# A vision tower kernel: three groups of images in its triangular solves, their later columns on POOL, and the layer norms of one phase applied by ACT

## The chip, the cores and the metric

The kernel runs on one core of one Trainium2 chip. The metric is the device time of one execution in microseconds (us), as the median of several runs; less is better. The core has five engines that run side by side and meet only at semaphores: TensorE (PE; its weight loads are PEld), VectorE (DVE), ScalarE (ACT), GpSimd (POOL) and SyncE (SP, which here only issues DMAs). Each takes its own instructions strictly in order, so an instruction that waits holds up everything behind it on its engine.

## What is computed

64 images of 36 patches and a class token, so 37 tokens each, of width 256, go through an embedding, multi-query attention, an entmax-gated two-layer product network (`cp_mumoe`), a delta-rule attention and a mixture of 8 experts, each behind a layer norm:

```python
h = _L0_tok_ref(x, ...)
h = h + _L0_attn_ref(_layernorm(h), ...)
h = h + _L0_ffn_ref(_layernorm(h), ...)
h = h + _L1_attn_ref(_layernorm(h), ...)
h = h + _L1_ffn_ref(_layernorm(h), ...)
```

The part that the change touches is in `_L1_attn_ref`. For each image and each of two heads it needs the inverse of a unit lower triangular matrix of 37x37:

```python
A0 = jnp.tril(-(jnp.einsum('bhnid,bhnjd->bhnij', k_beta, k) * L[None, :, None]), -1)
M = eye - A0
A = solve_triangular(M, jnp.broadcast_to(eye, M.shape), lower=True, unit_diagonal=True)
v = A @ v
```

There are 128 such systems, one for an image and a head.

## The kernel before

Tokens are handled in tiles of three images (111 rows of SBUF), 22 tiles in 11 pairs. The phases run one after the other: embedding and first attention in turns over the pairs; the entmax gates; a **merged phase**; an **attended phase**, in the same block without a barrier; routing; and the experts.

A turn i of the merged phase runs, over a pair of tiles, the two-layer product network of pair i, its output and the statistics of the norm for pair i-1 (`add_outputs`), POOL's power for the norm (`power_rows`), the norm itself (`normalise`, on VectorE, L1319), the transposes, and for pair i-2 the products of the delta rule: `decay_products` on VectorE (L1328, L1333) writes the masked system of a tile, and `fold` on POOL (L1528, L1529) brings it to 111x74. VectorE begins a turn with `gate_second` and `gate_first` (L1291, L1283). SP stores every folded tile to DRAM (`n_rows`, L970).

The systems are solved by **groups** of images (`GROUPS`), since a solve wants one system to a partition and so needs a trip through DRAM: `load_systems` brings the folded systems of a group to `sys_n`, VectorE solves them into `sys_x` by forward substitution, `store_inverses` (L1000) writes the inverses to DRAM and `load_inverses` (L1008) brings them back in the layout of tiles. There are two groups, pairs 0 to 5 and 6 to 10, and one place for both. `sets` is the number of times that the systems of a group fit in 128 partitions: with two sets, each partition solves every second column of the inverse.

`substitution` (L1340) is a generator that emits one matrix row i of the solve at a time: a product of the finished part of each column with row i (L1383), then a reduce (L1390). Columns are cut in two parts, early and late, each with its own semaphore, and the products of both stand ahead of the reduces of both. `advance` puts rows between the other work of VectorE until an estimated cost, `SLOTS`, is used up. Group 0 is solved within merged turns 8 to 12, and is drained there before the last decay products. Group 1 is solved within the attended phase, and drained before tile 12.

In the attended phase, turn t runs on TensorE `solve_values(t)` (L1130, the inverse of tile t by its values), `read_out(t-1)`, `turn_outputs(t-3)`, `attend(t)` and `router_logits(t-3)`. `solve_values(t)` needs `spread_inverses(t)` of POOL (L1537), which needs the loaded inverses. VectorE adds the result to the tokens and takes the statistics (`add_read`, L1417 to L1425), POOL raises to the power -0.5 (`power_outputs`, L1547), and VectorE applies the norm (`normalise_outputs`, L1432) at the head of its turn. SP stores the finished tiles to `x_rows`. SP's queue also carries the expert weights: 8 MB to `arena_w1` behind the first `load_inverses`, and 4 MB to half of `arena_w2` behind the second.

The buffers of these phases are carved out of two arenas, `arena_w1` and `arena_w2`, and of `work`; the names in the rows are those of the arenas.

## Time and profile before

| what | value |
|---|---|
| median of 3 runs | 836.15 us (834.35 to 836.52) |
| the profiled execution | 836.92 us, its span 835.1 us |
| PE, PEld busy | 678.3 us (81%), 519.5 us (62%) |
| DVE, POOL, ACT busy | 448.1 us (54%), 260.3 us (31%), 229.1 us (27%) |
| mean granted clock of TensorE | 0.886 of full speed |

The page of the profile cuts the span in 40 slices of 20.9 us. Each digit is the busy share of an engine in tenths; PEclk is the granted clock of TensorE in tenths of full speed (2.4 GHz; 0.5 is 1.2 GHz):

```profile
PE   5899999999977149999983385196569999999994
DVE  1567777777765742444799199466613333333321
ACT  0223333333322043443431022032013232232321
POOL 2344444444441012455453122022012221222211
PEclk9899999999986558999997589578569999999998
```

The merged phase stands from slice 15 to slice 22, the attended phase in slices 23 to 28, and the experts behind slice 30. A time in a row of the trace is in us from the start of the span.

### The profile page before, as it was taken

How to read it: one execution, taken by the hardware profiler on the slowest of the kernel's cores; microseconds unless marked ns; L12 is line 12 of the kernel's file. 1: busy time of each engine (PE TensorE's matmuls, PEld its weight loads, DVE VectorE, ACT ScalarE, POOL GpSimd, SP SyncE). 2: the span in 40 equal slices, each digit the busy share in tenths (PEclk: the TensorE clock that was granted, in tenths of full speed). 3: DMA queues.
4: the chain of work that ended last, by engine and by line, in shares of the span. 5: the costliest groups of instructions: out<-in, count | busy, mean ns of one | idle time of the engine just before them, and what ended most of it. 6: DMA issues, size and time to landing. Idle time of an engine off the chain costs nothing. (4 is left out here: it accounts for less than half of the span.)

```text
span 835.1 us, 13690 instructions
## 1 busy us (share of the span) xinstructions
PE 678.3 (81%) x4562; PEld 519.5 (62%) x4562; DVE 448.1 (54%) x1266; ACT 229.1 (27%) x635; POOL 260.3 (31%) x418
## 2 busy tenths in 40 slices
PE   5899999999977149999983385196569999999994
PEld 4567677777755139999972364085436767667673
DVE  1567777777765742444799199466613333333321
ACT  0223333333322043443431022032013232232321
POOL 2344444444441012455453122022012221222211
PEclk9899999999986558999997589578569999999998
DMA  8211111111000000000100670193411111111110
GB/s 303 93 35 34 34 35 34 34 35 33 2 2 1 0 2 0 7 7 6 25 7 4 171 303 1 27 356 96 196 50 39 57 47 50 57 44 52 51 32 20
DMA packets 24643, 49.77 MB, mean 60 GB/s; under 512 B 15284, under 2 KB 15414, under 8 KB 23936
## 3 DMA queue, kind: packets, MB, share of 16 engines
q1 hardware_dynamic: 20960, 34.43, 12.7%
q0 software_dynamic: 3328, 10.23, 4.0%
q10 hardware_dynamic: 288, 4.25, 1.3%
q8 instruction: 39, 0.64, 0.3%
q14 instruction: 28, 0.23, 0.1%
HBM read 39.03 MB, written 9.86 MB: 59 GB/s over the span
## 5 line engine op out<-in xcount | busy, mean ns | idle before, releaser
L1762 PE MATMUL psum<-arena_w,work 128*128 x208 | 95.9, 605 | 1.0 <-DVE work L1814 1.0
L1860 ACT ACTIVATE work<-psum,cst 128x128 f32<-128x128 f32 x208 | 56.6, 383 | 144.1 <-PE psum L1775 144.1
L1786 PE MATMUL psum<-arena_w,work 128*128 x416 | 94.2, 379 | 0.4 <-ACT work L1860 0.4
L1786 PEld LDWEIGHTS psum<-arena_w,work 128*128 128x128 f32 x416 | 77.1, 190 | 10.5 <-issue 1.1
L1724 POOL DMA_INDIRECT out<-work,row_i x26 | 25.8, 990 | 160.2 <-DVE work L1836 160.2
L1823 DVE COPY work<-psum 128x512 f32<-128x512 f32 x52 | 36.0, 692 | 70.0 <-PE psum L1762 61.9
L346 PE MATMUL psum<-arena_w 128*111 128x256 f32 x264 | 64.1, 396 | 4.9 <-DMA arena_w<-in_pack 4.9
L1762 PEld LDWEIGHTS psum<-arena_w,work 128*128 128x128 f32 x208 | 38.3, 194 | 40.1 <-issue 40.1
L711 POOL TENSOR_TENSOR arena_w<-arena_w,work 101x592 f32<-101x592 f32 x33 | 39.6, 1200 | 72.2 <-DVE work L577 72.2
L346 PEld LDWEIGHTS psum<-arena_w 128*111 128x111 f32 x264 | 46.5, 183 | 19.7 <-issue 9.6
L1130 PE MATMUL psum<-tokens,work 111*111 111x128 f32 x88 | 18.2, 340 | 43.4 <-POOL work L1537 43.4
L1830 DVE TENSOR_TENSOR tokens<-psum,cst 128x256 f32<-128x256 f32 x26 | 11.0, 425 | 73.6 <-PE psum L1786 73.6
L702 POOL TENSOR_TENSOR arena_w<-arena_w 128x296 f32<-128x296 f32 x66 | 44.0, 689 | 20.7 <-DVE arena_w L545 20.7
L400 PE MATMUL psum<-arena_w 128*37 128x296 f32 x264 | 41.3, 434 | 3.3 <-ACT arena_w L665 3.3
L1130 PEld LDWEIGHTS psum<-tokens,work 111*111 111x111 f32 x88 | 13.7, 216 | 44.6 <-POOL work L1537 33.0
L1069 PE MATMUL psum<-arena_w 128*128 128x222 f32 x176 | 40.9, 379 | 0.5 <-DVE arena_w L1283 0.5
L634 ACT COPY arena_w<-psum 37x592 f32<-37x592 f32 x33 | 25.2, 765 | 58.1 <-PE psum L411 58.1
L557 DVE TENSOR_REDUCE work<-psum 101x16 f32<-101x592 f32 x33 | 25.4, 771 | 24.1 <-PE psum L400 24.1
L1069 PEld LDWEIGHTS psum<-arena_w 128*128 128x128 f32 x176 | 34.3, 202 | 5.3 <-issue 3.0
L1717 POOL DMA_INDIRECT tokens<-x_rows,row_i x26 | 25.5, 980 | 36.5 <-SPq L174 28.9
L411 PEld LDWEIGHTS psum<-cst,arena_w 101*128 101x128 f32 x264 | 26.4, 148 | 16.8 <-POOL arena_w L711 9.1
L432 PE MATMUL psum<-arena_w 37*32 37x74 f32 x1056 | 24.9, 231 | 13.5 <-DVE arena_w L568 12.2
(216 smaller groups left out, 1344.6 us busy)
## 6 DMA issues: line engine op xcount, KB each, us to landing
arena_w<-in_w SPq DMA_DIRECT2D x2, 4096.0 KB, 13.3
arena_w<-in_x SPq DMA_DIRECT2D x22, 333.0 KB, 2.9
x_rows<-tokens SPq DMA_DIRECT2D x22, 192.0 KB, 5.7
arena_w<-in_pack ACTq DMA_DIRECT2D x1, 2420.0 KB, 10.9
cst<-in_packc ACTq DMA_DIRECT2D x1, 1727.0 KB, 14.9
arena_w<-in_pack SPq DMA_DIRECT2D x1, 818.5 KB, 7.3
arena_w<-in_pack SPq DMA_DIRECT2D x2, 384.0 KB, 4.6
work<-a_rows SPq DMA_DIRECT2D x21, 32.4 KB, 2.0
```

Source lines behind the costliest of these rows:

```text
L346: mm = nc.tensor.matmul(bank[0][0:R, j * D:(j + 1) * D], xp[j][:, k * R:(k + 1) * R], w_lin[:, k, :], start=(k == 0), stop=(k == PC - 1))
L400: mm = nc.tensor.matmul(bank[4 + f][e * HP:e * HP + TOK, 0:HH * TOK], qt[:, a:a + TOK], kb[p % 2 * 2 + e], start=True, stop=True)
L411: mm = nc.tensor.transpose(turns_bank[:, c * 128:c * 128 + PR], prob[p % 2][:, c * 128:(c + 1) * 128], ident[0:PR, 0:PR])
L702: nc.gpsimd.tensor_tensor(kb[p % 2 * 2 + e].rearrange("p (h s) -> p h s", h=HH), kt[:, a:a + TOK].unsqueeze(1).broadcast_to([128, HH, TOK] ...
L711: nc.gpsimd.tensor_tensor(by_head(prob[p % 2], HP), by_head(prob[p % 2], HP), small[p % 2][:, 2 * NH:3 * NH].unsqueeze(2).broadcast_to([PR ...
L1069: mm = nc.tensor.matmul(bank[2 + f // 2 % 2][:, (f % 2) * W:(f % 2 + 1) * W], w_out1[:, f, :], z1, start=True, stop=True)
L1130: mm = nc.tensor.matmul(bank[t % 2][0:R, h * 128:(h + 1) * 128], ab[t % 2][:, h * R:(h + 1) * R], x_half(t)[:, h * 128:(h + 1) * 128], sta ...
L1724: pool.indirect_dma_start(out_h, bass.IndirectOffsetOnAxis(ap=row_i[:, 2 * i + j:2 * i + j + 1], axis=0), yo[j], None).then_inc(y_stored[j ...
L1762: mm = nc.tensor.matmul(bank[2 * j + f][:, :], xgt[j][:, k * 128:(k + 1) * 128], arena_w1[:, bass.ds(expert * (2 * FF) + (k * FF + f * 512 ...
L1786: mm = nc.tensor.matmul(bank[7][:, 0:D], ht[j][:, g * 128:(g + 1) * 128], arena_w2[:, bass.ds(expert * (FC * D) + g * D, D)], start=(g == ...
L1823: nc.vector.tensor_copy(hp[j][:, f * 512:(f + 1) * 512], bank[2 * j + f][:, :]).then_inc(h_out[j], 1)
L1860: nc.scalar.activation(ht[j][:, g * 128:(g + 1) * 128], bank[4 + f][:, k * 128:(k + 1) * 128], ACT.Gelu, bias=cst[:, bass.ds(expert * FC + ...
```

## The change

- `GROUPS` has three groups: pairs 0 to 4, 5 to 7 and 8 to 10 (30, 18 and 16 images; 2, 2 and 4 sets). Each has a place of its own (`place_of`), so a solve need not wait until the group before it has been stored.
- The columns of a solve are cut at column 16. The earlier ones stay on VectorE, as products and reduces of one part only. The later ones are solved on POOL by columns: for each i from 16 on, a product of the solved x[i] with column i of the system and an addition to all the later rows. Both engines call the same `substitution`, each with its own semaphore; `solved` of a group is complete when both have reported.
- `SLOTS` has new budgets, three for VectorE and two for POOL, with a new estimate of a row's cost. POOL must empty its queue before it spreads the first tile of a group.
- Both norms are applied by ACT, as x times a scale plus a bias; POOL makes the bias (minus mean times scale) behind its power. VectorE keeps the statistics.
- SP stores and reloads group 0 ahead of the stores of tiles 19 to 21, and group 1 ahead of the 8 MB of weights. The loaded inverses lie in `arena_w2`.

```diff
-GROUPS = ((0, 6), (6, PAIRS))
-SLOTS = (1.0, 1.0, 5.0, 1.7)
+GROUPS = ((0, 5), (5, 8), (8, PAIRS))
+SLOTS = (1.0, 5.5, 1.0, 4.0, 1.2)
...
+            def substitution(eng, ops, g, which):
...
+                for i in range(which * split * sets, TOK - which):
+                    most = min(cols, i // sets + 1)
+                    c0, c1 = (split, most) if which else (0, min(split, most))
+                    if c0 >= c1 or i == which == 0:
+                        continue
+                    j0, j1 = (i + 1, TOK) if which else (0, i + 1)
...
+                    free(eng, chain[which], steps[which])
+                    if which:
+                        ops.tensor_tensor(w, x[:, c0:c1, i:i + 1].broadcast_to(shape),
+                                          n[:, j0:j1, i].unsqueeze(1).broadcast_to(shape), ALU.mult).then_inc(chain[which], 1)
+                        eng.wait_ge(chain[which], steps[which] + 1)
+                        ops.tensor_tensor(x[:, c0:c1, j0:j1], x[:, c0:c1, j0:j1], w, ALU.add).then_inc(chain[which], 1)
+                    else:
+                        ops.tensor_tensor(w, x[:, c0:c1, j0:j1], n[:, i, j0:j1].unsqueeze(1).broadcast_to(shape),
+                                          ALU.mult).then_inc(chain[which], 1)
+                        eng.wait_ge(chain[which], steps[which] + 1)
+                        ops.tensor_reduce(x[:, c0:c1, i], w, AX_X, ALU.add).then_inc(chain[which], 1)
...
-                    if g:
-                        store_inverses(g - 1)
+                        if t == NT - NB and g == LAST > 0:
+                            store_inverses(0)
+                            load_inverses(0)
                     load_systems(g)
-                for g in range(LAST):
+                for g in range(1, LAST):
+                    store_inverses(g)
                     load_inverses(g)
...
+                        last = nc.scalar.activation(xn[i % 2][:, j * D:(j + 1) * D], h_pair(i)[:, j, :], ACT.Identity,
+                                                    bias=st1[:, 16 + j:17 + j], scale=st1[:, 14 + j:15 + j])
...
                 for t in range(NT + 3):
                     copy_solved(t)
+                    normalise_outputs(t - 2)
                     copy_turned(t - 3)
                     copy_attended(t)
...
                 for t in range(NT + 3):
-                    if t == firsts[LAST]:
-                        advance(math.inf)
-                    normalise_outputs(t - 2)
+                    turn_no[0] = PAIRS + 2 + t
+                    while t in firsts and len(queue) > LAST - firsts[t]:
+                        solve_some(0.1)
                     add_read(t - 1)
                     keep_logits(t - 3)
                     if t > 0:
-                        advance(SLOTS[3])
+                        solve_some(SLOTS[2])
...
                 for t in range(-2, NT + 1):
                     power_outputs(t - 1)
+                    if t + 2 in firsts:
+                        take_up(math.inf, firsts[t + 2])
+                        while queue:
+                            solve_some(0.1)
                     spread_inverses(t + 2)
+                    take_up(PAIRS + 2 + t)
+                    solve_some(SLOTS[4])
```

How the rows of the solve now stand on VectorE, at the end of group 0 in merged turn 10. Before, two rows of the solve (each two products, then two reduces; 72 partitions):

```order
L1383 TENSOR_TENSOR work<-arena_w 72x560
L1383 TENSOR_TENSOR work<-arena_w 72x361
L1390 TENSOR_REDUCE arena_w<-work 72x16
L1390 TENSOR_REDUCE arena_w<-work 72x19
L1383 TENSOR_TENSOR work<-arena_w 72x576
L1383 TENSOR_TENSOR work<-arena_w 72x400
L1390 TENSOR_REDUCE arena_w<-work 72x16
L1390 TENSOR_REDUCE arena_w<-work 72x20
```

Now (124 partitions, two sets), followed by the decay products:

```order
L998 TENSOR_TENSOR work<-arena_w 124x288
L1001 TENSOR_REDUCE arena_w<-work 124x8
L998 TENSOR_TENSOR work<-arena_w 124x296
L1001 TENSOR_REDUCE arena_w<-work 124x8
L1401 TENSOR_TENSOR arena_w<-psum,arena_w 111x222
```

The late part has left VectorE, so each product is followed at once by the reduce that needs it.

POOL between the last fold of the merged phase and the first spread of an inverse (`spread_inverses`, 111x222). Before:

```order
L1528 TENSOR_TENSOR arena_w<-arena_w 111x74
L1529 TENSOR_TENSOR arena_w<-arena_w 111x74
L1537 TENSOR_TENSOR work<-work,arena_w 111x222 x3
```

Now, where "..." leaves out eleven pairs of the same kind:

```order
L1553 TENSOR_TENSOR arena_w<-arena_w 111x74
L993 TENSOR_TENSOR work<-arena_w 100x52
L996 TENSOR_TENSOR arena_w<-arena_w,work 100x4x13
...
L993 TENSOR_TENSOR work<-arena_w 100x10
L996 TENSOR_TENSOR arena_w<-arena_w,work 100x10
L1005 ISA
L1561 TENSOR_TENSOR work<-arena_w 111x222 x3
```

Thirteen rows of group 1 and the mark that it is solved (L1005) have moved between the two.

POOL in attended turn 8, between the power of tile 7 (L1572) and the spread of tile 10. Before, the power and the spread stood next to each other, as in every turn:

```order
L1547 TENSOR_TENSOR work<-work 111x1
L1537 TENSOR_TENSOR work<-work,arena_w 111x222
```

Now, where "..." leaves out nine pairs:

```order
L1572 TENSOR_TENSOR work<-work 111x1
L1573 TENSOR_SCALAR work<-work 111x1
L993 TENSOR_TENSOR arena_w<-arena_w 128x33
L996 TENSOR_TENSOR arena_w<-arena_w 128x3x11
...
L993 TENSOR_TENSOR arena_w<-arena_w 128x5
L996 TENSOR_TENSOR arena_w<-arena_w 128x5
L1005 ISA
L1561 TENSOR_TENSOR work<-arena_w 111x222
```

Eleven rows of group 2 stand ahead of the spread of the first tile of group 1.

## Rows read from the trace of the kernel before

**Rows 1.** Busy by stretch: PE, PEld, DVE, ACT, POOL, PEclk, DMA share, GB/s.
```profile
440.00:474.00 34.00, 8.48 (x30) 5.92 (x30) 21.84 (x54) 3.00 (x15) 10.55 (x26) 0.61 0.22 42
```

**Rows 2.** Timeline (start, us, engine, line, [idle <-releaser]): attended phase begins.
```profile
473.54 1.16 PE L1130 MATMUL psum<-tokens,work 111*111 111x128 f32 x4 [11.28 <-POOL work L1537]
...
478.96 1.00 DVE L1417 SCALAR_TENSOR_TENSOR tokens<-psum,arena_w,tokens 111x256 f32<-111x256 f32 x2 [15.73 <-PE psum L1151]
```

**Rows 3.** Timeline: the trip of the second group's inverses, SP and TensorE.
```profile
531.18 2.01 SPq L1000 DMA_DIRECT2D a_rows<-arena_w  x4
538.20 3.31 SPq L1008 DMA_DIRECT2D work<-a_rows  x7
...
540.63 0.88 PEld L1130 LDWEIGHTS psum<-tokens,work 111*111 111x111 f32 x4 [25.19 <-POOL work L1537]
```

**Rows 4.** Timeline: VectorE, starts of merged turns and fixed work in one.
```profile
388.43 0.45 DVE L1291 SCALAR_TENSOR_TENSOR arena_w<-psum,arena_w 128x222 f32<-128x222 f32 x1 [4.25 <-PE psum L1081]
...
400.13 0.45 DVE L1291 SCALAR_TENSOR_TENSOR arena_w<-psum,arena_w 128x222 f32<-128x222 f32 x1 [4.24 <-PE psum L1081]
...
415.00 0.37 DVE L1328 TENSOR_TENSOR arena_w<-psum,arena_w 111x222 f32<-111x222 f32 x1
...
417.57 0.40 DVE L1383 TENSOR_TENSOR work<-arena_w 72x90 f32<-72x90 f32 x2
...
438.38 0.43 DVE L1291 SCALAR_TENSOR_TENSOR arena_w<-psum,arena_w 128x222 f32<-128x222 f32 x1
```

**Rows 5.** Timeline: VectorE, solve rows with one part and with two (x2).
```profile
409.63 0.19 DVE L1383 TENSOR_TENSOR work<-arena_w 72x36 f32<-72x36 f32 x1
...
410.15 0.21 DVE L1383 TENSOR_TENSOR work<-arena_w 72x49 f32<-72x49 f32 x1
...
528.36 0.73 DVE L1383 TENSOR_TENSOR arena_w<-arena_w 120x288 f32<-120x288 f32 x2
...
529.63 0.74 DVE L1383 TENSOR_TENSOR arena_w<-arena_w 120x296 f32<-120x296 f32 x2
```

**Rows 6.** Groups: line, engine, op, shapes, count | busy us, mean ns | idle.
```profile
L1383 DVE TENSOR_TENSOR arena_w<-arena_w 120x296 f32<-120x296 f32 x1 | 0.5, 457 | 0.0
...
L1432 DVE TENSOR_SCALAR tokens<-tokens,work 111x256 f32<-111x256 f32 x22 | 11.0, 502 | 16.6 <-POOL work L1547 16.6
...
L1319 DVE TENSOR_SCALAR arena_w<-tokens,arena_w 111x256 f32<-111x256 f32 x22 | 8.1, 411 | 5.9 <-POOL arena_w L1489 5.9
...
L1237 ACT COPY tokens<-psum 111x256 f32<-111x256 f32 x22 | 8.1, 366 | 0.0
```

**Rows 7.** Timeline: POOL, short operations of one merged turn.
```profile
332.14 0.20 POOL L1514 TENSOR_TENSOR arena_w<-arena_w 111x2 f32<-111x2 f32 x1
...
333.30 0.31 POOL L1528 TENSOR_TENSOR arena_w<-arena_w 111x74 f32<-111x74 f32 x1 [0.53 <-DVE arena_w L1333]
333.69 0.33 POOL L1529 TENSOR_TENSOR arena_w<-arena_w 111x74 f32<-111x74 f32 x1
```

**Rows 8.** Timeline: a VectorE product of the solve, and POOL beside it.
```profile
449.69 1.01 DVE L1383 TENSOR_TENSOR work<-arena_w 72x512 f32<-72x512 f32 x2
449.86 0.90 POOL L1515 TENSOR_TENSOR arena_w<-arena_w 111x2 f32<-111x2 f32 x1
```

**Rows 9.** Timeline: VectorE, one turn of the attended phase up to its solve.
```profile
498.51 1.00 DVE L1417 SCALAR_TENSOR_TENSOR tokens<-psum,arena_w,tokens 111x256 f32<-111x256 f32 x2
...
500.37 0.33 DVE L1383 TENSOR_TENSOR arena_w<-arena_w 120x51 f32<-120x51 f32 x2
```

**Rows 10.** Timeline: VectorE, add_read behind the restart, and the last two.
```profile
548.11 1.00 DVE L1417 SCALAR_TENSOR_TENSOR tokens<-psum,arena_w,tokens 111x256 f32<-111x256 f32 x2 [1.36 <-PE psum L1151]
...
552.64 1.00 DVE L1417 SCALAR_TENSOR_TENSOR tokens<-psum,arena_w,tokens 111x256 f32<-111x256 f32 x2 [1.36 <-PE psum L1151]
...
574.02 0.99 DVE L1417 SCALAR_TENSOR_TENSOR tokens<-psum,arena_w,tokens 111x256 f32<-111x256 f32 x2
...
576.88 1.00 DVE L1417 SCALAR_TENSOR_TENSOR tokens<-psum,arena_w,tokens 111x256 f32<-111x256 f32 x2
```

More of the change, by code:

```diff
@@ L952, in group_of, with place_of, products_of @@
                 return im0, im1, nb, stride, 128 // stride
+            def place_of(g):
+                if g == LAST:
+                    return (arena_w2[:, k * TOK * TOK:(k + 1) * TOK * TOK] for k in range(2))
+                if g == 0:
+                    return sys_n, sys_x
+                return (arena_w1[:, k * TOK * TOK:(k + 1) * TOK * TOK] for k in range(2))
+            def products_of(g):
+                space = arena_w2[:, 2 * TOK * TOK:] if g == LAST else work
+                return space[:, 0:16 * TOK], space[:, 16 * TOK:16 * TOK + 21 * 21]
             def systems_of(rows, g, h):
@@ new lines, in advance @@
+            def advance(queue, budget, fixed, each):
+                while queue and budget > 0:
+                    size = next(queue[0], None)
+                    if size is None:
+                        queue.pop(0)
+                    else:
+                        budget -= fixed + each * size
+            steps = [0, 0]
+            begun = {}
+            ends = {GROUPS[g][1] - 1: g for g in range(len(GROUPS))}
+            firsts = {2 * GROUPS[g][0]: g for g in range(len(GROUPS))}
@@ L1393, in substitution @@
-                    for which in range(2):
-                        dve.wait_ge(chain[which], steps[which])
-                    nc.vector.engine_nop().then_inc(solved[g], 1)
-                pending = [None]
-                def advance(budget):
-                    while pending[0] is not None and budget > 0:
-                        cost = next(pending[0], None)
-                        if cost is None:
-                            pending[0] = None
-                        else:
-                            budget -= cost
+                    nc.vector.memset(rows_n[:, 0:TOK * TOK:TOK + 1], 1.0).then_inc(diagonal[g], 1)
@@ L1408, in add_read, with solve_some, all_steps @@
+                    dve.wait_ge(diagonal[g], 1)
+                queue = []
+                turn_no = [0]
+                def solve_some(budget):
+                    advance(queue, budget, 0.3, 0.0021)
+                def all_steps(g):
+                    begun[g] = turn_no[0]
+                    prepare(g)
+                    yield 700
+                    yield from substitution(dve, nc.vector, g, 0)
                 def add_read(t):
@@ L1546, in power_outputs, with solve_some, take_up, all_steps @@
                     pool.wait_ge(vare2, t + 1)
-                    tt(ve2[t % 2][:, 1:2], ve2[t % 2][:, 0:1], halves[:, 0:1], ALU.pow).then_inc(powered2, 1)
+                    free(pool, normed2, t - 1)
+                    link(tt(ve2[t % 2][:, 1:2], ve2[t % 2][:, 0:1], halves[:, 0:1], ALU.pow))
+                    ts(ve2[t % 2][:, 2:3], st2[t % 2][:, 6:7], ve2[t % 2][:, 1:2], -1.0, ALU.mult, ALU.mult).then_inc(powered2, 1)
+                queue = []
+                def solve_some(budget):
+                    advance(queue, budget, 0.5, 0.0042)
+                taken = []
+                def take_up(turn, most=LAST):
+                    for g in range(most + 1):
+                        if g not in taken and begun[g] < turn:
+                            taken.append(g)
+                            queue.append(all_steps(g))
+                def all_steps(g):
+                    pool.wait_ge(diagonal[g], 1)
+                    yield from substitution(pool, nc.gpsimd, g, 1)
                 ends_of_groups = [2 * p1_ - 1 for _, p1_ in GROUPS[:LAST]]
```

145 lines of the change are left out of this document (59 added, 86 removed).

## The prediction, before the changed kernel was run

> **What bounds the kernel now.** I read the busy table by stretches first, then the engines in order of time with what ended their idle time. TensorE fills most of the span, but two holes stand in it. From 440 to 474 us it works 8.48 of 34 us at a granted clock of 0.61 [rows 1]; the last part of that hole ends with the first multiplication of the attended phase at 473.54, after 11.28 us of waiting for POOL [rows 2]. The second hole is the longer: 25.19 us, again ended by POOL's spread inverses [rows 3]. In both, POOL itself waits: for VectorE to finish a triangular solve and for its result to go to DRAM and back. That trip is in [rows 3]: stores issued at 531.18, loads at 538.20, TensorE going again at 540.63, so 9.4 us from solved to working. In between, VectorE sets the pace. A merged turn takes 11.70 us where TensorE bounds it (388.43 to 400.13); the next three, with a solve in them, take 38.25 us together, 3.15 more than three such turns [rows 4].
>
> **What the solve costs on VectorE.** Before, a row of the solve has two independent parts (early and late columns), so each covers the other's latency. A row with one part runs product, reduce, next product strictly in turn: 0.52 us for 36 elements (409.63 to 410.15) [rows 5]. The product alone grows from 0.19 us at 36 elements [rows 5] to 0.457 at 296 [rows 6], 0.00103 us an element. A row with one part of n elements is then 0.45 + 0.00206 n us. A row with both parts, 288 and 200 elements, took 1.27 us [rows 5]; the same row with its first part alone comes to 0.45 + 0.59 = 1.04. The change takes 41% of that row's elements away from VectorE and, by this, 18% of its time. On short rows it saves nothing.
> Two groups before: 12472 and 6653 elements, both parts counted, come with 0.25 us a row (what is left of 1.27 after 488 x 0.0021) to about 36 and 24 us. After: 36 rows in each of three groups with 5315, 5315 and 2687 elements in the first part, so 27.1, 27.1 and 21.7 us, 76 against 60. The norms give back 8.1 + 11.0 = 19.1 us [rows 6]. VectorE's total load stays nearly level; what can be won is only the place of the work and the two trips to DRAM.
>
> **The norms on ACT.** Nearest row: an ACT copy of 111x256 at 0.366 us [rows 6]; 44 of them are 16 us on an engine that worked 3.00 of 34 us [rows 1]. They stand behind a wait for POOL's power in ACT's order, with the GELUs of the turn's second half queued behind. The two new POOL scalings cost about 0.3 us each with their gap [rows 7]. I count this at nothing: between 0 (VectorE's slack covers it) and 0.5 us for each of 11 turns.
>
> **The merged phase after.** POOL's part of a solve is 20 rows of two operations. Start to start POOL needs 0.39 us for 74 elements and about 0.28 for 2 (0.20 and the 0.08 gap seen behind the larger) [rows 7]: 0.275 + 0.0016 n, so 0.68 us a row at 43 elements, 13.6 us for a group of 30 or 18 images, 12.5 for the last. The Trainium skill (Perfetto Trace Analysis, GPSIMD Engine Instruction) says to time POOL by such spacing and not by reported durations; by the durations alone the row would be 0.5 us and the drains below a quarter shorter.
> VectorE's fixed work in a turn: gates 0.7, first decay products and outputs with their statistics 2.57 (415.00 to 417.57) [rows 4], second decay products 0.8 (estimate from the 0.37 of one and two smaller), 4.1 in all. The order puts 14, 11, 9 and 13 rows of the solve into turns 7 to 10, and two preparations of 1.3 us. That is 13.0, 12.8, 12.7 and 13.1 us, all above 11.7. To turns 9, 10 and 11 I add 0.7 each for the shared port: [rows 8] show POOL's 2-element product, 0.20 us elsewhere, taking 0.90 while a VectorE product of 512 elements ran. From 388.4 this leads to 441 for turn 11 (before 438.4), and with its 12 rows to 455. The last decay products then wait for POOL's strengths, which stand behind seven of POOL's solve rows; I put their end at 462, before 463.2. Almost no gain here.
> The trip of group 0 leaves early: POOL marks it solved behind its inverses of turn 11, at about 453.5, so its inverses are back at 463. But POOL does not spread them: its order empties the queue first, 13 rows of group 1 behind the last fold. 462 + 0.8 + 13 x 0.68 + 1.4 of port waits + 0.6 for the spread is 465 + 9: TensorE starts at **474**, against 473.54 [rows 2]. One wait takes the other's place.
>
> **The attended phase after.** The first add_read came 5.4 us after the start (478.96 after 473.54) [rows 2], so now at 479.4. A turn of VectorE is 1.86 us of add_read and logits [rows 9] plus its solve rows; the order gives 2, 2, preparation, 4, 4, 3, 3, 3 in turns 1 to 8: 28.7 us. In POOL's turn 8 stands the second drain: 11 rows of group 2, 7.3 us, ahead of the spread of tile 10. Tile 9's add_read comes 12.4 us behind tile 7's, not 7.2: 5.2 us lost. Then 16.4 us to tile 14 and 5.6 for the last rows; with 1 us for a lowered clock the last group is solved at 479.4 + 25.1 + 12.4 + 16.4 + 5.6 + 1 = 540. Eight smaller stores instead of four: I keep the 9.4 us of [rows 3], so TensorE restarts at **549**, 8.7 us later than before (540.63), with six tiles left and not ten.
> From a restart at the low clock turns take 4.53 us (548.11 to 552.64), later 2.86 (574.02 to 576.88) [rows 10], of which 0.3 was the norm in VectorE's chain: 2.7 now. Last add_read before: 36.25 us behind the restart. After: 3 + 2 x 4.53 + 4 x 2.7 = 22.9, so 571.9 against 576.88. The remaining path is unchanged. **Gain 5 us.** The profiled execution took 836.92 us (span 835.1), 0.8 above the median of 836.15; 831.9 for it, **831** for the median.
>
> **Bounds of what no row shows.** POOL's rows with broadcast, strided operands: from 0.5 us (durations) to 0.9 (each product behind half a VectorE product) instead of 0.68; 24 of them lie on the path, -4 to +5 us. The trip with eight stores: 7 to 12 us, -2 to +3. ACT's norms: 0 to +4.
>
> **Rivals.**
> The drains are hidden. If POOL runs well ahead in the merged phase, TensorE starts when group 0's inverses are back, 465, and the stall before tile 10 shrinks to 2 us: another 12 us, 819. For it: POOL works only 10.55 of 34 us in [rows 1]. Against: in the order both drains stand squarely ahead of the spreads, and the last fold cannot come before VectorE's decay products.
> The port decides. In [rows 8] we see a short POOL operation held for nearly all of a VectorE product. If each meeting is paid in full, VectorE loses a POOL operation, 0.28 us, for each of 27 rows in the merged turns (7.6, of which 2.1 are counted), and the 24 drained rows 0.2 to 0.3 more each: 5.5 + 6 us, and the result is 842, slower. It turns from gain to loss at 5 us of such waits. For it: now both engines run two-input products at once for some 40 us. Against: reduces, half of VectorE's rows, held nothing in these rows. The Trainium skill (SBUF — State Buffer, Who interferes with whom) has this as an exclusive lock: two-input VectorE operations and POOL's reads block each other for the whole instruction, reduces never do. The held operation agrees.
> Nothing comes of it. The last group's turns run 0.3 us slower each than I sum, and the restart is at 553: 835 to 838. A lowered clock through the attended phase does this too; [rows 1] show 0.61 behind a hole.
>
> **How the numbers follow.** Forecast 831 (825 to 834), 0.52; hidden drains 0.15; nothing 0.17; the port 0.16. About 0.3%, 2.5 us, can be told from no change: faster below 833.6, slower above 838.7. Some of the forecast's upper end belongs to no change: faster 0.66, same 0.17, slower 0.17. Range 821 to 840.
>
> **What would show it.** Right: merged turns of 13 us from turn 7; a POOL stretch of product and sum rows of 9 to 11 us just before its first spread, TensorE's first attended work at 474 +/- 3; a hole of 4 to 6 us before tile 10; a hole of about 14 us before tile 16 that ends near 549; single-part solve rows of 0.45 us plus size. Wrong: TensorE starting at 465 (drains cheap), VectorE products well above 0.46 us beside POOL (the port), or GELUs of the second half waiting for ACT's norm by more than 0.5 us a turn.

## The result, and the profile of the changed kernel

| | before | changed |
|---|---|---|
| median of 20 runs, us | 835.06 (830.57 to 836.71) | 839.56 (834.80 to 840.88) |
| ratio | | 1.0046, 95% interval 1.0031 to 1.0061 |
| profiled execution (span), us | 836.92 (835.1) | 839.81 (837.9) |
| busy VectorE, POOL, ACT, us | 448.1, 260.3, 229.1 | 431.4, 302.5, 246.7 |

The change makes the kernel 0.46% slower, where the forecast said 0.6% faster. Of its 20 executions 4 took 834.8 to 835.8 us and 16 took 838.0 to 840.9; the profiled one is of the second kind. Three moments of the trace carry what follows: TensorE's first attended work, the last add_read, and the issue of the next phase's weights, which marks the end of the attended phase.

VectorE's gate_second starts the merged turns, as in [rows 4]. Timeline of the changed kernel, VectorE (start, us, engine, line, operands, what ended its idle time):
```profile
389.43 0.45 DVE L1377 SCALAR_TENSOR_TENSOR arena_w<-psum,arena_w 128x222 f32<-128x222 f32 x1 [4.02 <-PE psum L1147]
...
394.05 0.09 DVE L1427 MEMSET arena_w<- 128x37 f32 x1 [2.38 <-DMA arena_w<-n_rows]
...
398.99 0.57 DVE L1406 SCALAR_TENSOR_TENSOR arena_w<-psum,arena_w 111x111 f32<-111x111 f32 x2 [1.86 <-POOL arena_w L1539]
...
406.68 0.44 DVE L1377 SCALAR_TENSOR_TENSOR arena_w<-psum,arena_w 128x222 f32<-128x222 f32 x1
...
413.38 0.57 DVE L1406 SCALAR_TENSOR_TENSOR arena_w<-psum,arena_w 111x111 f32<-111x111 f32 x2 [1.85 <-POOL arena_w L1539]
...
420.98 0.44 DVE L1377 SCALAR_TENSOR_TENSOR arena_w<-psum,arena_w 128x222 f32<-128x222 f32 x1
```
The first turn with a solve takes 17.25 us and not 13.0. Two waits stand in it: 2.38 us in the preparation, for the loads of group 0's systems, and 1.86 us before the second decay products, for POOL's strengths. The next turn takes 14.30, with the second wait again.

The preparation stood at the head of a turn in the kernel before too, and did not wait. VectorE before, and SyncE's loads of group 0's systems after:
```profile
401.56 1.20 DVE L1351 MEMSET arena_w<- 128x1369 f32 x1 [0.23 <-issue]
402.86 0.09 DVE L1356 MEMSET arena_w<- 128x37 f32 x1
```
```profile
388.92 1.67 SPq L1046 DMA_DIRECT2D arena_w<-n_rows  x4
```
Before, two loads were issued from 399.02, 1.1 us ahead of the turn that begins at 400.13, and VectorE went on with the decay products at 403.02. Now there are four, from 388.92, 0.5 us ahead of the turn at 389.43, and VectorE goes on at 394.05, 5.1 us behind the first issue.

POOL ahead of the first spread, and TensorE behind it, the counterpart of [rows 2]; timelines of POOL, TensorE and VectorE:
```profile
470.79 0.47 POOL L993 TENSOR_TENSOR work<-arena_w 100x52 f32<-100x52 f32 x1
471.35 0.29 POOL L996 TENSOR_TENSOR arena_w<-arena_w,work 100x52 f32<-100x52 f32 x1
471.71 0.43 POOL L993 TENSOR_TENSOR work<-arena_w 100x60 f32<-100x60 f32 x1
...
481.01 1.08 POOL L1561 TENSOR_TENSOR work<-arena_w 111x222 f32<-111x222 f32 x2 [0.15 <-POOL arena_w L996]
...
481.72 1.16 PE L1196 MATMUL psum<-tokens,work 111*111 111x128 f32 x4 [12.71 <-POOL work L1561]
...
487.14 1.00 DVE L1452 SCALAR_TENSOR_TENSOR tokens<-psum,arena_w,tokens 111x256 f32<-111x256 f32 x2 [11.12 <-PE psum L1217]
```
From 470.79 to 481.01 POOL does nothing but group 1's rows, 13 of them; the loads of group 0's inverses had been issued from 468.12 on, as the next lines show. TensorE starts 8.2 us later than before (473.54).

SyncE's queue through the attended phase, the counterpart of [rows 3], with TensorE's restart and VectorE's last work of the phase:
```profile
461.22 2.06 SPq L1064 DMA_DIRECT2D a_rows<-arena_w  x4
468.12 5.48 SPq L1072 DMA_DIRECT2D arena_w<-a_rows  x11
...
548.52 3.67 SPq L1064 DMA_DIRECT2D a_rows<-arena_w  x8
553.54 2.81 SPq L1072 DMA_DIRECT2D arena_w<-a_rows  x6
...
555.92 1.19 PE L1196 MATMUL psum<-tokens,work 111*111 111x128 f32 x4 [11.29 <-POOL work L1561]
...
556.39 0.46 SPq L1093 DMA_DIRECT2D arena_w<-in_w  x1
556.89 26.76 SPq L1097 DMA_DIRECT2D x_rows<-tokens  x44
...
582.22 0.17 DVE L1467 TENSOR_TENSOR work<-psum,cst 111x8 f32<-111x8 f32 x1 [1.65 <-PE psum L1236]
...
586.97 0.35 SPq L1643 DMA_DIRECT2D arena_w<-in_w  x1
```
All 44 stores of x_rows stand in SyncE's order behind the last group's inverses and 4 MB of weights. They are issued until 583.65, so VectorE's last work of the phase (582.22) is not its end: the next phase begins at 586.97. The last add_read was at 575.71 (before 576.88, [rows 10]), so 1.2 us were won up to there, and 4.6 lost behind it.

The attended phase holds one thing more, the turns behind the hole before tile 10; VectorE's add_reads:
```profile
525.24 1.00 DVE L1452 SCALAR_TENSOR_TENSOR tokens<-psum,arena_w,tokens 111x256 f32<-111x256 f32 x2 [6.62 <-PE psum L1217]
...
529.77 1.00 DVE L1452 SCALAR_TENSOR_TENSOR tokens<-psum,arena_w,tokens 111x256 f32<-111x256 f32 x2 [0.72 <-PE psum L1217]
...
534.30 1.00 DVE L1452 SCALAR_TENSOR_TENSOR tokens<-psum,arena_w,tokens 111x256 f32<-111x256 f32 x2 [1.50 <-PE psum L1217]
...
537.26 0.99 DVE L1452 SCALAR_TENSOR_TENSOR tokens<-psum,arena_w,tokens 111x256 f32<-111x256 f32 x2
```
Two turns take 4.53 us each, and the granted clock of TensorE is 0.50 from 525.2 to 534.3; then 2.96. In the traces of e2 and e7 below, which have the same hole of 10.1 us, the same two turns take 3.71 and 2.9 us at a granted clock of 0.97 and 0.96. So behind the same hole the clock differs from trace to trace, and 2.4 us between two of these traces can be the clock alone.

### The profile page after: what moved, and what is told of

Read it like the earlier page. It is cut to its first block and busy times, and to the rows that moved or that the text cites. A ratio compares the mean times of both kernels' runs of the same rounds, so it can differ in the third digit from the quotient of the medians.

```text
span 837.9 us, 13862 instructions
## 1 busy us (share of the span) xinstructions
PE 675.0 (81%) x4562; PEld 515.0 (61%) x4562; DVE 431.4 (51%) x1186; ACT 246.7 (29%) x679; POOL 302.5 (36%) x582
## 5 line engine op out<-in xcount | busy, mean ns | idle before, releaser
L1196 PE MATMUL psum<-tokens,work 111*111 111x128 f32 x88 | 17.6, 332 | 31.5 <-POOL work L1561 31.5
L634 ACT COPY arena_w<-psum 37x592 f32<-37x592 f32 x33 | 25.2, 763 | 57.9 <-PE psum L411 57.9
L1452 DVE SCALAR_TENSOR_TENSOR tokens<-psum,arena_w,tokens 111x256 f32<-111x256 f32 x44 | 21.2, 483 | 36.4 <-PE psum L1217 35.6
L411 PEld LDWEIGHTS psum<-cst,arena_w 101*128 101x128 f32 x264 | 26.2, 148 | 16.7 <-POOL arena_w L711 9.5
```

The costliest lines, as they stand in the source:

```text
L411: mm = nc.tensor.transpose(turns_bank[:, c * 128:c * 128 + PR], prob[p % 2][:, c * 128:(c + 1) * 128], ident[0:PR, 0:PR])
```

## The experiments

The ratio is that of each kernel to the kernel before, run beside it, with its 95% interval. The three last columns are from the profiled execution of each, counted from its first gate_second of the merged phase (before 320.69, changed 319.83), so that what happened earlier does not enter: TensorE's first attended work, the last add_read, the end of the phase. "Less" and "more" below are differences of medians, against the 839.56 of the changed kernel where nothing else is named. The kernels were run at different times, so where such a difference is small the two ratios and their intervals decide. The profiled execution of e1 is its fastest, 823.78, 4.5 us below its median.

| run | median us | ratio | attended start | last add_read | end |
|---|---|---|---|---|---|
| before | 835.06 | 1 | 152.9 | 256.2 | 262.9 |
| changed | 839.56 | 1.0046 (1.0031 to 1.0061) | 161.9 | 255.9 | 267.1 |
| e1 | 828.24 | 0.9909 (0.9888 to 0.9930) | 156.8 | 242.5 | 253.8 |
| e2 | 835.69 | 0.9996 (0.9976 to 1.0015) | 161.7 | 252.8 | 260.8 |
| e3 | 837.19 | 1.0021 (1.0002 to 1.0039) | 158.2 | 257.3 | 264.1 |
| e4 | 817.21 | 0.9784 (0.9761 to 0.9808) | 150.0 | 235.2 | 246.5 |
| e5 | 827.32 | 0.9915 (0.9892 to 0.9938) | 157.3 | 245.1 | 254.4 |
| e6 | 833.23 | 0.9982 (0.9965 to 0.9999) | 161.4 | 248.7 | 257.3 |
| e7 | 836.94 | 1.0040 (1.0023 to 1.0057) | 161.0 | 252.6 | 264.1 |
| e8 | 820.45 | 0.9834 (0.9813 to 0.9855) | 157.9 | 239.1 | 247.1 |
| e9 | 818.79 | 0.9801 (0.9787 to 0.9814) | 157.8 | 237.0 | 246.0 |
| e10 | 818.85 | 0.9801 (0.9786 to 0.9815) | 150.5 | 238.5 | 246.2 |
| e11 | 817.26 | 0.9775 (0.9750 to 0.9800) | 150.4 | 235.1 | 243.1 |
| e12 | 821.27 | 0.9839 (0.9824 to 0.9854) | 149.9 | 240.1 | 246.8 |
| e13 | 831.61 | 0.9960 (0.9941 to 0.9979) | 162.4 | 249.3 | 257.3 |
| e14 | 821.75 | 0.9840 (0.9826 to 0.9853) | 151.6 | 238.8 | 248.4 |
| e15 | 835.44 | 0.9999 (0.9989 to 1.0009) | 157.5 | 253.7 | 261.6 |

**e1, POOL's drains.** POOL empties its queue only up to the group that is about to be spread.
```diff
-                        while queue:
+                        while len(queue) > len(taken) - 1 - firsts[t + 2]:
                             solve_some(0.1)
```


> The changed kernel, but POOL empties its queue of solve rows ahead of a spread only as far as the group that is spread: group 1's rows no longer stand before the first spread (10.1 us from 470.79 to 480.9), group 2's no longer before tile 10 (6.9 us from 514.6). Theory A, the place of these rows in POOL's order is what costs: TensorE starts its attended work when group 0's inverses are back, 472 instead of 481.7, the hole before tile 10 falls to about 2 us, the last group is solved some 8 us earlier, and the time falls from 839.6 to about 831. Rival B, the rows cost as much wherever they stand (shared port, blocked products): the attended turns grow by what the drains gave, and the time stays within 2 us of 839.6.

Measured 828.24, 11.3 us less. The hole before tile 10 (10.10 us between two add_reads) is gone. The attended start moves by 5.1 us only, not 9.7: in POOL's order six rows of group 1 remain ahead of the first spread, those of its last merged turn. This is A, and 3 us more than it said: the two turns of 4.53 us are also absent from this trace. Without the drains the change is a gain of 0.9%, with them a loss of 0.5%.

**e2, stores earlier.** SyncE stores 12 tiles before it waits for the last group.
```diff
+                store_rows(range(12))
                 store_inverses(LAST)
                 load_inverses(LAST)
...
-                for t in range(NT):
+                store_rows(range(12, NT))
```


> The changed kernel, but SyncE stores the first 12 tiles of x_rows before it waits for the last group's solve, not after it and after the 4 MB of weights. Theory A, the last 4 us of the attended phase (last VectorE work 582.4, next phase 587.0) belong to this backlog of 44 stores: the phase ends at about 583 and the time falls by 4 us to 835.5. Rival B, the weights' own 4 MB or the last stores end it anyway: less than 1 us.

Measured 835.69, 3.9 us less, as A said; from the last add_read to the end it is 8.0 us, not 11.3. The last add_read is earlier too in this trace, by 3.1 us, and 2.4 of that is the clock (see above).

**e3, norms back on VectorE.** Both norms as in the kernel before.
```diff
+                    normalise(i - 1)
                     decay_products(i - 2, 1)
...
+                    normalise_outputs(t - 2)
                     add_read(t - 1)
```


> The changed kernel with both norms back on VectorE (0.50 us x 2 a merged turn, 0.41 us an attended turn), all else kept, three groups and POOL's columns too. Theory A, the norms on ACT are a gain where VectorE is late: four solving turns of the merged phase grow by 1 us each, 22 attended turns by 0.2 to 0.4, and the time rises by 4 to 8 us to 844 to 848. Rival B, ACT's norm costs more than it gives (11.85 us a turn instead of 11.70 where no solve runs, and a longer chain power, scaling, norm in each attended turn): the time falls by 1 to 4 us.

Measured 837.19, 2.4 us less: B, though only just, since the two ratios' intervals touch (1.0002 to 1.0039 and 1.0031 to 1.0061). The turns without a solve are 11.70 and not 11.85 us, and the first two gate_seconds stand 9.23 apart, not 10.35: 2 us before any solve. But the norm here also stands between the two decay products, where the changed kernel waits for POOL; e6, e12 and e15 tell this apart.

**e4, POOL's rows left out.** The later columns are not computed; POOL only marks them as solved.
```diff
-                for i in range(which * split * sets, TOK - which):
+                for i in range(which * split * sets, 0 if which else TOK):
```


> The changed kernel without POOL's share of the solve: the later columns are not computed, POOL only marks them done; VectorE's rows are all there. It gives the whole price of POOL's rows, their place in the order and their use of the shared port together. Theory A (place in the order): the time is at most 3 us below that of the kernel in which only the drains are put right, near 829. Theory B (the port): it is 8 us or more below it, and VectorE's solving turns of the merged phase fall from 14.3 and 14.6 us to 13 or less.

Measured 817.21, 11 us below e1, which A did not allow. But B's sign is missing: the merged turns take 17.41, 14.30, 14.19 and 14.06 us, against 17.25, 14.30, 14.63 and 14.66. POOL's rows lengthen a merged turn by 0.6 us at most, and VectorE's wait before the second decay products is 1.86 us without them too. What else made the 11 us was open; the waits in both traces pointed to the mark. SyncE's queue, the store of group 0's inverses, in e1 and then in e4:
```profile
458.32 2.06 SPq L1064 DMA_DIRECT2D a_rows<-arena_w  x4
```
```profile
453.59 2.16 SPq L1064 DMA_DIRECT2D a_rows<-arena_w  x4
```
Counted from the first gate_second (317.12 and 319.48) these are 141.2 and 134.1.

**e5, marked at once.** On top of e1, the mark stands behind the last row, not at the queue's next advance.
```diff
+                    if i == TOK - 1 - which:
+                        eng.wait_ge(chain[which], steps[which])
+                        ops.engine_nop().then_inc(solved[g], 1)
                     yield (c1 - c0) * (j1 - j0)
-                eng.wait_ge(chain[which], steps[which])
-                ops.engine_nop().then_inc(solved[g], 1)
```


> The kernel with the drains put right (828.2 us) and one thing more: each engine marks its share of a group as solved right behind its last row. Before, the mark came only when the queue was next advanced, on POOL a whole turn behind the last row (last row of group 0 ended at 449.0 in that trace, SyncE's stores followed at 458.3). Theory A, this late mark makes most of the 11 us between that kernel and the one without POOL's rows (817.2): stores of group 0 at about 451, TensorE's attended start 7 us earlier, time 820 to 822. Rival B, the difference is POOL's rows themselves (the port, and rows drained later beside VectorE): time within 2 us of 828.

Measured 827.32, B's time: theory A falls. The store now leaves at 454.27 (135.5 from the first gate_second, 5.7 earlier), and TensorE starts no earlier. POOL's timeline shows why:
```profile
469.81 0.33 POOL L1554 TENSOR_TENSOR arena_w<-arena_w 111x74 f32<-111x74 f32 x1
470.10 0.46 POOL L993 TENSOR_TENSOR work<-arena_w 100x52 f32<-100x52 f32 x1
...
475.11 0.30 POOL L996 TENSOR_TENSOR arena_w<-arena_w,work 100x56 f32<-100x56 f32 x1
475.37 0.56 POOL L1562 TENSOR_TENSOR work<-arena_w 111x222 f32<-111x222 f32 x1
```
The last fold is at 469.81, and six rows of group 1 (5.3 us) still stand between it and the spread. The trip through DRAM had not been what POOL waited for.

**e14, the last slot too.** As e5, and POOL takes no rows in its last merged turn.
```diff
-                    solve_some(SLOTS[3])
+                    if i <= PAIRS:
+                        solve_some(SLOTS[3])
```


> The kernel that marks at once (827.3 us) without POOL's own six rows at the end of its last merged turn (5.3 us of POOL just ahead of the first spread, 470.1 to 475.4 in that trace). Theory A, these rows took the place of the late mark: TensorE's attended work starts at 470.5 to 471 instead of 476.1, and the time falls by 4 to 6 us to about 822, near the 817.2 of the kernel without POOL's rows. Rival B, the shared port is the rest: less than 2 us gained.

Measured 821.75, 5.6 us less than e5: A. The attended start is at 151.6, against 150.0 without POOL's rows. So of the 11 us between e1 and e4, 6.5 are the place of POOL's marks and rows, and some 4.5 are left for the rows themselves, the port among them. That last figure is loose: by the ratios it is 4.7 us with about 2 either way, and in the two traces the phase ends only 1.9 us apart.

**e6, solve rows between.** VectorE's rows of a merged turn are split about the second decay products.
```diff
-SLOTS = (1.0, 5.5, 1.0, 4.0, 1.2)
+SLOTS = (1.0, 3.6, 1.0, 4.0, 1.2)
...
                     add_outputs(i - 1)
+                    solve_some(1.9)
                     decay_products(i - 2, 1)
```


> The changed kernel (839.6 us) with about four solve rows of each merged turn moved on VectorE to stand between the outputs and the second decay products, as such rows and the norm did in the kernel before; the rest of the rows follow as now. Theory A, the merged turns with a solve are long (14.3, 14.6 us against the 12.8 I summed) because VectorE idles 1.9 us there for POOL's strengths: those turns take 12.5 to 13 us and the time falls by 4 to 6 us to about 834.5. Rival B, POOL only reaches its strengths later because VectorE's rows stand ahead of its norm inputs or hold the port: turns stay at 14 us or more, time within 1.5 us of 839.6.

Measured 833.23, 6.3 us less: the size is A's, the path only half. The first two turns with a solve fall to 15.21 and 12.79 us and the fourth to 13.99, but the third grows to 15.37, since the first decay products now come before POOL's strengths. Timeline of VectorE in e6:
```profile
420.83 0.38 DVE L1401 TENSOR_TENSOR arena_w<-psum,arena_w 111x222 f32<-111x222 f32 x1
422.95 0.57 DVE L1406 SCALAR_TENSOR_TENSOR arena_w<-psum,arena_w 111x111 f32<-111x111 f32 x2 [1.74 <-POOL arena_w L1540]
```
POOL's seven solve rows of the turn before stand ahead of those strengths. The four turns together are 3.5 us shorter, yet the attended start is unchanged (161.4). Each of the two slots rounds up to a whole row, so VectorE does six rows more of group 1 ahead of its last decay products (up to the product of 256 elements, in the changed kernel up to 208), and POOL's last fold comes where it was: 150.1 from the first gate_second, in the changed kernel 150.7. The gain comes behind the start: the rows of groups 0 and 1 are done before the first add_read, the last group is begun earlier and solved 9.2 us earlier (540.44, counted from the first gate_second 219.5 against 228.7), and both holes shrink, from 10.10 to 7.36 and from 15.60 to 12.92 us.

**e7, preparation later.** Group 0 is prepared behind the second decay products of its turn.
```diff
-                    solve_some(SLOTS[0])
+                    if i - 3 != GROUPS[0][1] - 1:
+                        solve_some(SLOTS[0])
...
-                    solve_some(SLOTS[1])
+                    solve_some(SLOTS[1] + (1.8 if i - 3 == GROUPS[0][1] - 1 else 0))
```


> The changed kernel with the preparation of group 0 moved on VectorE from the head of turn 7 to behind that turn's second decay products, with the same number of rows behind it. In the changed kernel VectorE stands 2.4 us there for the loads of the systems while TensorE waits for its decay products (the turn takes 16.9 us). Theory A: the turn takes 14.5 us and the time falls by 2.4 us to 837.2. Rival B: the wait was covered, the turn keeps 16 us or more, time within 1 us of 839.6.

Measured 836.94, 2.6 us less in the medians, but the ratios, 1.0040 and 1.0046, have intervals that almost coincide: no gain is shown. The turn falls by 1.55 us to 15.70, between what A and B said, and turn 9 grows from 14.63 to 15.32, so the four turns are 0.8 us shorter together. Of the 3.0 us between the two traces at the phase's end, 2.4 is the clock.

**e13, the last three together.** e2, e6 and e7 in one, the drains kept.

> The changed kernel with the three things that the forecast had not priced taken away together (rows between outputs and second decay products, group 0 prepared late, 12 tiles stored early), POOL's drains kept. Theory A, they lie one behind the other on the path: 839.6 - 6.3 - 2.6 - 3.9 = 826.8. Rival B, the waits overlap (the earlier merged turns only lengthen POOL's drain, whose rows are then all still ahead of it): 831 or more.

Measured 831.61, 8.0 us less: B. The gains overlap. The attended start is at 162.4, where it was. The four merged turns are 2.5 us shorter, but the last fold is no earlier (151.0 from the first gate_second, 150.7 in the changed kernel): as in e6 VectorE has done more rows ahead of its last decay products. POOL's 13 rows follow the fold as before:
```profile
469.96 0.33 POOL L1561 TENSOR_TENSOR arena_w<-arena_w 111x74 f32<-111x74 f32 x1
470.24 0.57 POOL L993 TENSOR_TENSOR work<-arena_w 100x52 f32<-100x52 f32 x1
470.89 0.29 POOL L996 TENSOR_TENSOR arena_w<-arena_w,work 100x52 f32<-100x52 f32 x1
...
480.59 1.08 POOL L1569 TENSOR_TENSOR work<-arena_w 111x222 f32<-111x222 f32 x2 [0.15 <-POOL arena_w L996]
...
481.30 1.16 PE L1201 MATMUL psum<-tokens,work 111*111 111x128 f32 x4 [14.13 <-POOL work L1569]
```

**e8, all five together.** e5, e2, e6 and e7 in one kernel (e5 holds e1).

> The changed kernel with all of it: POOL empties its queue only as far as needed, marks at once, rows between outputs and second decay products, group 0 prepared late, x_rows of 12 tiles stored before SyncE waits for the last group. If the parts are independent and lie on one path: 839.6 - 11.3 (drains) - 7 (marks) - 5 (rows between) - 2.4 (preparation) - 3.9 (stores) = 810. If they overlap, since VectorE's load of 76 us of solve stays: 815 to 818.

Measured 820.45, 1.7% faster than before, but short of the sum by 10 us and of the cautious range by 2: the parts overlap more than either said.

**e9 to e11, where the rows go.** e9 is e8 with more rows in each attended turn; e10 is e9 with the rows ahead of the last decay products and of the first spread taken out; e11 is e10 with more rows still.
```diff
-SLOTS = (1.0, 3.6, 1.0, 4.0, 1.2)
+SLOTS = (1.0, 3.6, 1.6, 4.0, 2.0)
```


> The kernel with all five corrections (820.5 us) and one size changed: VectorE takes 1.6 instead of 1.0 of solve budget in an attended turn (3 rows instead of 2), POOL 2.0 instead of 1.2. In the trace of that kernel the last group is solved at 532.5, TensorE then stands 10 us for the trip through DRAM (add_reads 529.96 and 542.95). Theory A, the last hole costs its whole trip because the rows end only when the tiles before it are used up; rows taken two or three tiles earlier let tiles 13 to 15 cover the trip: hole 3 us or less, time 812 to 815. Rival B, VectorE's attended turns grow by just what is saved and the hole stays: within 2 us of 820.5.

Measured 818.79, within B's 2 us, though the hole is gone, as A said. Before tile 16 the largest gap is 4.53 us instead of 12.99, yet the last add_read comes only 2.1 us earlier: the attended turns have grown.

> As the kernel with 1.6 and 2.0 of budget, and besides no solve rows ahead of the last two decay products on VectorE (turn 12), half as many at the end of turn 11, and none of POOL's in its turn 12, ahead of the first spread (5.3 us, six rows, in the trace of the kernel that marks at once); the products get a place beside the router's logits, so that rows may run later. Theory A, after the drains were put right the attended start hangs on these rows: it moves from 17 us behind the inverses' store to 10, 5 to 7 us earlier, and since the rows left over run beside attended tiles the time falls by 3 to 6 us against the kernel without this. Rival B, VectorE's rows are only moved and the last group is solved later by as much: within 1.5 us.

Measured 818.85: B, though the attended start moves by 7.3 us, to 150.5. Rows not done by then are done later, a hole before tile 16 is back (8.39 us), and the last group is solved 0.5 us sooner at most.

> As the last, with 2.2 of budget for VectorE in an attended turn. Theory A: the hole before tile 16 is gone at 1.6 already and longer turns only delay the tiles before: 0 to 2 us slower. Rival B: the trip still shows at 1.6, and 2.2 gains 2 to 4 us more.

Measured 817.26, 1.6 us less than e10, where A had 0 to 2 more and B 2 to 4 less; the intervals of e10 and e11 overlap, so neither is shown. It is the fastest kernel of the study that computes everything: 0.9775 (0.9750 to 0.9800) of the kernel before, 2.2% faster.

**e12 and e15, the norms by themselves.** e12 is e10 with both norms back on VectorE, as in e3. e15 is the kernel before with both norms on ACT and nothing else changed.

> The kernel with corrections, 1.6 and 2.0 of budget and the free tail, with both norms back on VectorE. In the changed kernel this edit gave 2.4 us, but there the norm also covered the wait for POOL's strengths. Theory A, with that wait covered by solve rows the norms are worth having on ACT: the merged turns with a solve grow by 1 us each and the time rises by 3 to 6 us. Rival B, ACT's norm costs by itself (0.15 us in each merged turn without a solve, a longer chain in each attended turn): the time falls by 1 to 3 us.

> The kernel before with one part of the change alone: both norms applied by ACT, with POOL's scalings; two groups, all columns on VectorE, solve rows still standing between outputs and second decay products. Theory A, ACT's chain costs 0.15 us in each of 7 merged turns without a solve, and gives VectorE back 0.73 us in each turn with one and 0.4 in each attended turn with solve rows (44 norms, 19.1 us, of which VectorE's late turns are some 14): 3 to 6 us faster than before, 830 to 832. Rival B, what VectorE wins it waits for elsewhere: within 1.5 us of 835.5. Rival C, the longer chain power, scaling, norm costs in the last six attended turns: slower, 837 or more.

e12 measured 821.27, 2.4 us more than e10, in A's direction and short of its range. e15 measured 835.44, no change: B. In e15 the merged phase loses: 10.34 for 9.22 between the first two gate_seconds, 11.85 for 11.70 in each turn without a solve, and the turns with one 13.62, 13.11 and 13.39 for 13.05, 12.53 and 12.67. The attended phase wins 7.2 us (from start to last add_read 96.1 for 103.3), of which 1.8 is one turn of 4.53 us behind the restart where the kernel before has two; its end hands back 1.3: 8.0 us from last add_read to end, before 6.7. So the norm on ACT is a loss in the merged phase and a gain in the attended one; a kernel with the one and not the other was not run.

## Why the prediction was wrong

Its own sum for the profiled execution was 831.9; it took 839.81. Of these 7.9 us, 7.7 were lost up to the attended start, 3.9 won back up to the last add_read, and 4.6 lost behind it; the rest of the program was some 0.5 shorter.

- **Merged turns 7 to 10: 61 us, not 53 (turn 11 starts at 450.3 and not at 441; 1.0 of this was there at turn 7).** The step that failed is the count of VectorE's fixed work, 4.1 us a turn, and of its preparations, 1.3 us each, with no waits in them. The old order had solve rows and the norm between the first and second decay products [rows 4], and these covered POOL's power and strengths; the change takes both away. The price is 1.85 to 1.86 us in each of the four turns, 0.2 to 0.3 more before the first decay products of turns 9 and 10, and 2.38 once for loads that are now four and issued later against the turn: 10.3 us in all, while the rest of the four turns was 2.5 us shorter than I summed. 13.0 + 2.38 + 1.86 is the 17.25 measured. The diff showed that rows and norm were gone from between; I priced the instructions and not the waits they had covered. POOL's share by the port, 0.7 a turn in my sum, was 0.4 to 0.6 (e4).
- **From turn 11 to the attended start: 31.5 us, not 33.** The mechanism was right: POOL's 13 rows stood ahead of the spread, and took 10.2 us from 470.79 to 481.01, the 8.8 + 1.4 of the sum. That makes the attended start 481.7 for 474. I had called it "one wait takes the other's place"; e1, e5 and e14 show how deep this goes: drain, mark and last slot each have to go before the next one shows. The second drain took 6.9 us from 514.6 on, 7.3 forecast.
- **Attended start to last add_read: 94.0 us, not 97.9.** The drain before tile 10 is there (13.4 us between add_reads of tiles 7 and 9, 12.4 forecast). The trip with eight small stores took 7.4 us from first store to TensorE, not 9.4. The two turns of 4.53 us stood behind the hole before tile 10, where I had 1 us for the clock, and not behind the restart, where I had two of them: the first there took 2.76 (558.85 to 561.61). That the clock fell there and not here I can't explain, and e2 and e7 have it at neither place; this part of the sum came out near by luck.
- **Last add_read to the end: 11.3 us, not 6.7.** "The remaining path is unchanged" failed. With six tiles left at the restart and not ten, SyncE has less time for 44 stores and 4 MB behind the same wait. e2 gives the size: 3.9 us by the medians, 3.3 in the tail of its trace.

The waits are read from the trace, on the engine that sets the pace there; the runs show them less directly. e13 puts rows into them, prepares late and stores early, the drains kept, and takes 831.6 us, where the forecast was 831. But it does not get there by the forecast's path: its four merged turns are only 2.5 us shorter, its attended start is at 162.4 from the first gate_second, where the forecast had some 154, and it makes up for that behind the start. That the two times agree is in part luck. No run shows an attended start as early as 154 with the drains kept.

The **norms on ACT** were counted at nothing, with the bound of 0 to 4 us. The traces show 2 us lost in the merged phase before a solve begins. The sign that I had named, GELUs of the second half later by more than 0.5 us, is there in turn 7: the norm waits 3.17 us for POOL on ACT, and these GELUs begin 10.3 us into the turn, for 7.6 before; in a turn without a solve it is 0.4 us. The sizing row was wrong too: an ACT norm, whose scale and bias each come from a column of memory, takes 0.60 us, not the 0.37 of a copy. Groups of the changed kernel:
```profile
L1300 ACT ACTIVATE tokens<-tokens,work 111x256 f32<-111x256 f32 x22 | 13.2, 600 | 18.1 <-POOL work L1573 18.1
...
L1292 ACT ACTIVATE arena_w<-tokens,arena_w 111x256 f32<-111x256 f32 x22 | 12.0, 595 | 18.7 <-POOL arena_w L1511 18.7
```
The Trainium skill (ScalarE: Activation LUTs, What ACT_TABLE_LOAD costs) had this price: 186 ns and 0.833 ns an element, and some 93 ns for each such operand, which for 256 elements and two operands makes 585 ns, an estimate; the rows agree at 595 and 600. By that estimate the 44 norms are 26 us on ACT; the rows above have 25.2 busy, and my sum had 16.

Of the **rivals**, the port gave nearly the measured time, 842, and is not the reason: e4 and e14 leave some 4.5 us for all of POOL's rows, once they stand in the right place, the merged turns lose 0.4 to 0.6 each, and both drains took what the sum gave them. The hidden drains (819) describe what e14 (821.75) reaches with a corrected order. A slip of the prediction changes nothing of this: by its own figures VectorE's rows in the kernel before come to 35 and 23 us, not 36 and 24.

What stays open: e8 to e11 all come out at 817 to 820.5, wherever the rows stand, and I did not show what bounds these; VectorE's load is the guess, though its busy time fell by 16.7 us. And no complete kernel has three groups without POOL's columns (e4 leaves these out of the result) or POOL's columns in two groups, so what each of the two is worth by itself is not known.

## What to carry to other kernels

When a change moves work away from between two steps of a chain on another engine, look for what that work covered: the wait appears at its full size, 1.85 us a turn here. When a queue is "emptied before" something, ask for which item it has to be empty, and put marks where the work ends and not where the queue is next looked at; here that gave nothing by itself (e5), and 6.5 us with the rows behind it moved as well (e14). Follow the far end of each in-order queue: a wait that moves later by 8 us carries everything behind it. And compare two traces turn by turn with the granted clock beside them, since two turns at half the clock are 2.4 us here.

## What the runs showed of the hardware

A large POOL operation holds a small VectorE product. Timelines of VectorE and POOL in the changed kernel:
```profile
399.46 1.13 POOL L1520 TENSOR_TENSOR tokens<-tokens,arena_w 111x512 f32<-111x512 f32 x1 [0.35 <-ACT arena_w L1292]
...
399.86 0.76 DVE L998 TENSOR_TENSOR work<-arena_w 124x6 f32<-124x6 f32 x1
400.65 0.16 DVE L1001 TENSOR_REDUCE arena_w<-work 124x2 f32<-124x6 f32 x1
400.84 0.17 DVE L998 TENSOR_TENSOR work<-arena_w 124x8 f32<-124x8 f32 x1
```
The product of 6 elements takes 0.76 us beside POOL's sum of 512 and the next one, of 8, takes 0.17. It is the reverse of [rows 8], where POOL was held. In the drain the effect is smaller: POOL's product takes 0.41 to 0.48 us while VectorE solves, and 0.30 for about as many elements once VectorE has stopped (at 476.02):
```profile
475.26 0.48 POOL L993 TENSOR_TENSOR work<-arena_w 100x56 f32<-100x56 f32 x1
475.82 0.29 POOL L996 TENSOR_TENSOR arena_w<-arena_w,work 100x56 f32<-100x56 f32 x1
476.19 0.30 POOL L993 TENSOR_TENSOR work<-arena_w 100x49 f32<-100x49 f32 x1
```
The Trainium skill (SBUF — State Buffer, Who interferes with whom) has it that whichever of the two issues first keeps the shared pair for its whole instruction and the other stands still; these rows agree with both directions. In e13, where VectorE stops at 474.07, the product of 54 elements takes 0.31 (at 474.21), in the changed kernel 0.44 (at 474.37). What all of it costs here is within the some 4.5 us left between e4 and e14.
